# Graph layers of a GNN and expert kernel: node tiles taken in eleven alternating runs, and the weight products dealt out 4, 5, 5, 4

## The reference, cut to what matters

```python
dst = jnp.minimum((6250 * jax.random.uniform(key, (100000,)) ** 2.0).astype(jnp.int32), 49999)
_o = jnp.argsort(dst, stable=True)          # edges come sorted by destination
...
xs = x[src]
seg = dst * R + etype
sums = jax.ops.segment_sum(xs, seg, num_segments=N * R)
cnt = jax.ops.segment_sum(jnp.ones_like(xs[:, 0]), seg, num_segments=N * R)
mean = sums / jnp.maximum(cnt, 1.0)[:, None]
mean = mean.reshape(N, R, -1)
return x @ Wroot + b + jnp.einsum('nrd,rde->ne', mean, W)
```

## Time and profile before

| what | value |
|---|---|
| timed, median of 3 runs | 3500.47 us (3499.16 to 3519.07) |
| span of the profiled execution | 3064.4 us |
| timed median less the span | 436.1 us |
| PE, DVE, POOL busy | 2352.2, 1782.2, 1836.5 us |
| setup, to PE's first matmul of the first layer | 97.4 us |
| first graph layer, from there to its last means | 97.4 to 1191.0 |
| second graph layer, from its first gather to its last means | 1202.6 to 2280.0 |
| routing and experts | from 2280 to the end |

### The profile page before, as it was taken

The page is one execution under the profiler, slowest core; times in us unless marked ns, Lnnn a source line. Parts: engine busy times, 40 slices in busy tenths (PEclk is TensorE's granted clock), DMA queues, the critical chain, the costliest instruction groups (busy, mean ns, idle before and its releaser), DMA issues.

```text
span 3064.4 us, 82720 instructions
## 1 busy us (share of the span) xinstructions
PE 2352.2 (77%) x19212; PEld 1776.0 (58%) x19213; DVE 1782.2 (58%) x4944; ACT 1167.6 (38%) x2306; POOL 1836.5 (60%) x1908
## 2 busy tenths in 40 slices
PE   1456777778888887456777888888987189999999
PEld 0123444555666775123445556667776178888888
DVE  7434445555566664333445555656666278877777
ACT  5001223334445553011223344455542165655554
POOL 1777777766666553777777777666536623333333
PEclk9556789999999998557899999999995599999999
DMA  7343333333333321333343444333335432322222
GB/s 244 100 130 105 108 108 108 109 101 99 97 94 93 90 88 58 106 99 115 115 119 118 123 122 125 112 113 111 106 110 192 146 123 86 100 72 72 72 72 61
DMA packets 164416, 331.14 MB, mean 108 GB/s; under 512 B 35518, under 2 KB 101786, under 8 KB 164216
## 3 DMA queue, kind: packets, MB, share of 16 engines
q0 software_dynamic: 90864, 245.38, 26.9%
q1 hardware_dynamic: 39608, 41.02, 4.5%
q10 hardware_dynamic: 33872, 43.92, 4.5%
HBM read 283.29 MB, written 49.07 MB: 108 GB/s over the span
## 4 chain that ended last, share of the span: by engine, by line
PE 48%; POOL 24%; issue 15%; DVE 7%; DMA 3%; DVEq 2%; ACT 1%; POOLq 0%; SPq 0%; ACTq 0%
POOL ring L450 20%; PE more_banks L1254 15%; PE sum_banks L1392 8%; PE sum_banks L1234 7%; PE sum_banks L1235 5%; PE sum_banks L1382 4%; PE more_banks L1382 4%; POOL lot_in L470 3%; PE more_banks L1246 3%; DMA ring<-table,row_tab 2%; DVE sel L890 1%; DMA out<-edge_work,lot_ids 1%; PE more_banks L1366 1%; DVEq L881 1%; DVE weights L1072 0%
## 5 line engine op out<-in xcount | busy, mean ns | idle before, releaser
L450 POOL DMA_INDIRECT ring<-table,row_tab x1568 | 1509.2, 963 | 703.8 <-issue 339.0
L1254 PE MATMUL more_banks<-weights,stage 128*128 128x256 f16 x5292 | 846.9, 283 | 7.8 <-ACT stage L561 4.5
L589 ACT ACTIVATE stage<-sum_banks,inv 128x256 f16<-128x256 f32 x784 | 327.4, 471 | 815.5 <-DVE inv L923 398.7
L1254 PEld LDWEIGHTS more_banks<-weights,stage 128*128 128x128 f16 x5292 | 502.4, 101 | 144.9 <-issue 71.6
L1234 PE MATMUL sum_banks<-ring,sel 128*128 x1568 | 449.3, 287 | 161.1 <-DVE sel L890 84.2
L898 DVE TENSOR_SCALAR sel_more<-lane,win_off,key_tab 128x128 f16 x780 | 268.8, 345 | 443.4 <-SPq L355 371.2
L1234 PE MATMUL sum_banks<-ring,sel_more 128*128 x780 | 244.3, 314 | 350.0 <-DVE sel_more L898 193.8
L890 DVE SCALAR_TENSOR_TENSOR sel<-lane,win_off,key_tab 128x256 f16<-128x256 f16 x792 | 349.4, 482 | 240.4 <-PE more_banks L1254 235.8
L1235 PE MATMUL sum_banks<-ring,sel 128*128 x1568 | 448.7, 287 | 0.0
L561 ACT ACTIVATE stage<-more_banks 128x1024 f16<-128x1024 f16 x392 | 402.7, 1027 | 15.1 <-PE more_banks L1246 14.9
L1234 PEld LDWEIGHTS sum_banks<-ring,sel_more 128*128 x780 | 78.4, 100 | 529.7 <-issue 524.9
(11 more groups left out here) (287 smaller groups left out, 2763.0 us busy)
## 6 DMA issues: line engine op xcount, KB each, us to landing
ring<-table,row_tab POOLq DMA_INDIRECT x1568
weights<-L_ffn_W ACTq DMA_DIRECT2D x96, 178.5 KB
stage<-L_ffn_W ACTq DMA_DIRECT2D x16, 1024.0 KB, 5.5
edge_work<-lot_in SPq DMA_DIRECT2D x54, 260.0 KB, 2.7
table<-edge_work SPq DMA_DIRECT2D x7, 896.0 KB, 4.4
table<-edge_work ACTq DMA_DIRECT2D x49, 128.0 KB
out<-acc SPq DMA_DIRECT2D x6, 1024.0 KB
acc<-x SPq DMA_DIRECT2D x6, 896.0 KB, 11.0
```

The costliest lines, as they stand in the source:

```text
L450: pool.indirect_dma_start(ring_rows[:, b % RING, 0:2 * D], None, tables[layer], bass.IndirectOffsetOnAxis(row_tab[:, b:b + 1], 0)).then_in ...
L589: act.activation(mean16[:, slot, h, 0:D], ps_sum[slot][h][:, 0:D], ACT.Copy, scale=inv[:, ds(c * 2 + h, 1)]).then_inc(mean_high[layer], 1)
L1254: return [pe.matmul(ps_out[par], rows[:, xp * KD + k, :], w16[:, wp, k, r * D:(r + 1) * D], start=part == 0 and n == 0, stop=part == PARTS ...
```

## The change

1. **Order of tiles.** The tiles are placed in `acc` and in all later work in the order of eleven runs, low and high node numbers in turn. Each run's blocks are gathered as a range of their own; a block that straddles a border of runs is gathered twice, so there are 794 gathers instead of 784. In setup, two tables of 784 columns are copied run by run with eleven copies each on ACT, `free_meta` run by run with eleven operations on DVE, all at places read from registers. Loads of x, stores of `tables[0]` and of the output are cut at the borders.
2. **Products.** The 18 products are dealt 4, 5, 5, 4 over couples 2 and 3 of the next tile and couples 0 and 1 of the one after. The root parts come first. The wait for the means moves to the start of couple 2. Sums, ReLU and the stores of rows come one couple later.
3. **Register arithmetic.** `meta` holds `lo + 2`, called `need`; a gather b goes to slot (b + 2) % 16, so that `need & 15` is the slot. Semaphore values are masked before they are waited for. `lot_meta` becomes 16 bits wide.

```diff
+    RUNS = ((0, 1), (13, 25), (1, 2), (25, 32), (2, 4), (32, 38), (4, 7), (38, 43), (7, 10), (43, 49), (10, 13))
+    COUNT = len(RUNS)
+    AT = [sum(b - a for a, b in RUNS[:r]) for r in range(COUNT + 1)]
+    GATHERS = BLOCKS + COUNT - 1
+    MASK = (1 << (GATHERS + 3 * WINDOWS).bit_length()) - 1
+    PART_ORDER = [R * KD + k for k in range(KD)] + list(range(R * KD))
+    SHARES = (5, 4, 4, 5)
+    SPREAD = {4: (1, 1, 0, 1, 1), 5: (1, 1, 1, 1, 1)}
+    CUTS = (0, SHARES[2], SHARES[2] + SHARES[3], SHARES[2] + SHARES[3] + SHARES[0], PARTS)
...
# POOL
-                for b in range(BLOCKS):
+                for b in range(GATHERS):
...
-                    pool.indirect_dma_start(ring_rows[:, b % RING, 0:2 * D], None, tables[layer],
+                    pool.indirect_dma_start(ring_rows[:, (b + 2) % RING, 0:2 * D], None, tables[layer],
...
# ACT, in setup (and the same for key_tab)
+            for r in range(COUNT):
+                act.activation(row_tab[:, ds(run_to[r], BLOCKS)], row_src[:, ds(run_from[r], BLOCKS)], ACT.Copy).then_inc(tabs_set, 1)
+                act.wait_ge(tabs_set, r + 2)
...
# DVE, in setup
+            for r in range(COUNT):
+                link(v.tensor_scalar(free_row[:, ds(to[r], BLOCKS)], free_src[:, ds(of[r], BLOCKS)], run_steps[:, r:r + 1], run_end[:, r + 1:r + 2], ALU.add, ALU.min))
...
# DVE, more_blocks
-                        v.wait_ge(rows_ready[layer], block + 1)
+                        v.wait_ge(rows_ready[layer], (lo & MASK) + i + 3)
...
# DVE, tile_work
-                        if k == 1 and age == 2:
+                        if k == 2 and age == 2:
                             sums_out(t - 2, par)
...
# PE
-                            pe.wait_ge(more_ready[layer], since + i + 1)
-                            block = (lo + i + 2).with_bounds(min_val=0, max_val=BLOCKS - 1)
-                            add_block(to, flat(sel_more[:, ds(block & (RING - 1), 1), :]), block, False, True).then_inc(steps_done[layer], 1)
+                            pe.wait_ge(more_ready[layer], (since & MASK) + i + 1)
+                            add_block(to, flat(sel_more[:, ds((need + i) & (RING - 1), 1), :]), need + i + 2, False, True).then_inc(steps_done[layer], 1)
...
-                    if k == 0:
-                        parts = [(par, n) for n in range(PARTS - 5, PARTS)] if age == 2 else []
-                    else:
-                        parts = [(1 - par, n) for n in (range(0, 2), range(2, 8), range(8, 13))[k - 1]] if age > 0 else []
-                    spread = ((1, 1, 1, 1, 1), (0, 0, 0, 0, 2), (1, 1, 1, 1, 2), (1, 1, 1, 1, 1))[k]
+                    due = (k + 2) % STEPS
+                    of, enough = (par, age == 2) if k < 2 else (1 - par, age > 0)
+                    parts = [(of, n) for n in PART_ORDER[CUTS[due]:CUTS[due + 1]]] if enough else []
+                    spread = SPREAD[SHARES[k]]
...
+                    if k == 2 and age > 0:
+                        if age == 1:
+                            pe.wait_ge(w_split, layer + 1)
+                        pe.wait_ge(means_in[layer], t * STEPS)
...
-                        pe.wait_ge(rows_ready[layer], lo[j] + 2)
+                        pe.wait_ge(rows_ready[layer], need[j] & MASK)
...
-                    if k == 1 and age > 0:
-                        if age == 1:
-                            pe.wait_ge(w_split, layer + 1)
-                        pe.wait_ge(means_in[layer], t * STEPS)
```

More of the change, by code:

```diff
@@ L67, in build_program, with pieces, whole @@
     WAYS = CHUNK + 1
-    STORES = (TILES - 1) // 8 + 1
-    assert (TILES - 1) % 8 == 0
+    def pieces(first, last):
+        cuts = [(max(AT[r], first), min(AT[r + 1], last)) for r in range(COUNT)]
+        return [(a, b, ORDER[a]) for a, b in cuts if a < b]
+    def whole(first, last):
+        return [p for p in pieces(first, min(TAIL, last)) + pieces(max(TAIL + 1, first), last)]
+    STORES = len(whole(0, TILES)) + 1
     tables = [nc.dram_tensor(f"table{l}", [NP, 2 * D], f16, kind="Internal").ap() for l in range(2)]
@@ L467, in _ @@
                     t = c * CHUNK + i
-                    rows = LAST if t == TILES - 1 else P
+                    rows = LAST if t == TAIL else P
                     for k in range(2):
@@ L855, in _ @@
             v.memset(meta[0:1, 0:1, :], 0)
-            link(v.memset(meta[0:1, WINDOWS:, :], 0))
-            v.tensor_copy(meta[0:1, 0:WINDOWS, 0], lo)
+            link(v.memset(meta[0:1, WINDOWS:, :], 2))
+            for r in range(COUNT):
+                wins = slice(AT[r] * WPT, AT[r + 1] * WPT)
+                v.tensor_scalar(meta[0:1, wins, 0], lo[:, wins], run_shift[:, r:r + 1], 2.0, ALU.add, ALU.add)
+                last = AT[r + 1] * WPT
+                v.tensor_scalar(run_end[:, r + 1:r + 2], upto[:, last - 1:last], 2.0 * last, None, ALU.add)
             v.tensor_copy(meta[0:1, 1:WINDOWS + 1, 1], upto)
@@ L1013, in _ @@
                 v.memset(cells[:, 0:5, :], 0.0)
-            for i in range(CHUNK):
-                v.tensor_scalar(ids7[:, i:i + 1], part_no[:], float(i * P), None, ALU.add)
             v.tensor_scalar(valid, part_no[:], float(LAST), None, ALU.is_lt)
@@ L1176, in _ @@
         def _(pe):
-            pe.wait_ge(consts, 10)
+            pe.wait_ge(consts, 9)
             pe.wait_ge(wrong_ready, 1)
@@ L1199, in _ @@
             pe.wait_ge(later_ready, 1)
-            for a in range(2):
-                for q in range(Q):
-                    ins = pe.matmul(bank[4 + a][:, 0:WINDOWS], ones16[0:NAT, :], later[:, a, q, :], start=q == 0, stop=q == Q - 1)
+            for q in range(Q):
+                ins = pe.matmul(bank[4][:, 0:LOOKS], ones16[0:NAT, :], ends_later[:, q, :], start=q == 0, stop=q == Q - 1)
+            ins.then_inc(spans_ps, 1)
+            pe.wait_ge(later_ready, 2)
+            for q in range(Q):
+                ins = pe.matmul(bank[5][:, 0:WINDOWS], ones16[0:NAT, :], starts_later[:, q, :], start=q == 0, stop=q == Q - 1)
             ins.then_inc(spans_ps, 1)
@@ L1312, in _ @@
                 graph_tiles(pe, tile_work)
-                for n in range(PARTS - 5, PARTS):
+                for n in PART_ORDER[CUTS[2]:CUTS[3]]:
+                    product(1, n)
+                turn(COUPLES - 1, 1)
+                for n in PART_ORDER[CUTS[3]:]:
                     ins = product(1, n)[-1]
                 ins.then_inc(out_done[layer], 1)
-                turn(COUPLES - 1, 1)
+                for n in PART_ORDER[:KD]:
+                    product(0, n)
                 pe.wait_ge(means_in[layer], COUPLES)
@@ L1319, in _ @@
                     weights_spread(1)
-                for n in range(PARTS):
+                for n in PART_ORDER[KD:]:
                     ins = product(0, n)[-1]
```

231 lines of the change are left out of this document (162 added, 69 removed).

## The result

The changed kernel takes 3646.8 us (3635.76 to 3653.22, 4 runs) against 3508.1 for the kernel before, timed beside it: a ratio of **1.039 [1.036, 1.042], slower**. The forecast was 3545, at most 3625.

A forecast was written before the change was run, and what follows sets the result against it. Gathers at 1.25 us were taken to bound low tiles, PE's sequencer the later ones. Terms -30 - 10 - 69 + 136 + 15 + 3 = +45 on the median of 3500.5 gave 3545 us, range 3425 to 3625.

The forecast's parts named there:

- order, with its setup: Graph layers: ring's head start cuts waits for gathers, -30 and -10 us; copies ahead of first gather and matmul add +15.
- dealing of the products: Couples of each tile: dealing 4, 5, 5, 4 saves 0.7 us a tile, -69 us, ends -20 and -108.
- arithmetic, with the rest: PE's loop over more steps: longer turns cost +136 us, ends 0 and +230; tails of both layers +3.
- What lies around it, 436 us, is not touched: Time outside the profiled span of 3064.4 us: unchanged, so the +45 is added to the median of 3500.5.
- two more masks, and one more addition or none: Each turn of PE's loop: added instructions at 0.1 us each, +0.2 or +0.3; 780 x 0.2 = 156 us before hiding.
- rival B: PE's loop: additions don't combine as before, a turn is 0.3 us longer, 78 us more, 3623 us; chance 0.15.
- Rival A: PE's loop: sequencer runs ahead, arithmetic is hidden, none of the 136 us is paid, 3409 us; chance 0.18.
- rival C: PE's loop: half the arithmetic's tax is hidden in couples with queued products, 3477 us, about no change; chance 0.17.
- -0.7 us a tile: Couples 1 and 2 of a tile: saving from the new dealing, between 0.2 and 1.1 us.
- Over 98 tiles: All tiles of both layers: the dealing's saving a tile applied to each, -69 us in all.
- as much as that run now waits for gathers: Heavy runs: head start's gain capped by present waits, 9 + 25 = 34 us in low tiles; -30 taken.
- rival D: Order of tiles: ring's head start gives nothing and each border costs its gather, 3610 us; chance 0.08.

The follow-up runs named there:

- e13: e9 with maxima with 0 in place of PE's masks once a window and once a loop: 3093.1 us, ratio 1.009, quiet set.
- e14: e13 with the products dealt 4, 5, 5, 4: 3068.1 us, ratio 1.001 to the kernel before, quiet set.
- e6: Changed kernel with tiles in natural order and the products dealt as before: 3663.3 us, ratio 1.042, with pauses.
- e9: Kernel before with semaphore values masked outside the loops, PE's and DVE's turns kept at 10 and 7 instructions: 3535.9 us, ratio 1.021, with pauses.
- e16: The program of e9 run again in a quiet set: 3146.4 us, ratio 1.027 to the kernel before.
- e10: e9 with PE's turn of the loop at 13 instructions, as in the changed kernel: 3654.8 us, ratio 1.055, with pauses.
- e18: Changed kernel with all tiles in one run in natural order: 3228.2 us, ratio 1.053, quiet set.
- e11: e9 with DVE's turn of the loop at 9 instructions: 3548.3 us, ratio 1.025, with pauses.
- e17: The whole changed kernel run again in a quiet set: 3247.1 us, ratio 1.059 to the kernel before.
- e8: e7 with its tiles in natural order: 3535.7 us, ratio 1.006, with pauses.
- e7: Changed kernel with masks taken out of the two loops and one slot computed for both places, PE's turn 10 instructions: 3572.5 us, ratio 1.016, with pauses.
- e1: Kernel before with its three small integer tables 16 bits wide instead of 32: 3870.0 us, ratio 1.102, with pauses.

## Why the prediction was wrong

| term | forecast | with pauses | quiet |
|---|---|---|---|
| order, with its setup | -40 + 15 | +22 | +19 |
| dealing of the products | -69 | -35 | -25 |
| arithmetic, with the rest | +136 + 3 | about +150 | +187 |
| sum | +45 | +139 | +181 |

The last line and the first two are measured (the quiet dealing between e13 and e14, in a kernel with short turns); the third is what they leave, and e6 measures it directly with pauses (+149). Setup, read from PE's first matmul, is 22 us longer where 15 were forecast: some 15 come with the order and 8 with the arithmetic.

**The footing.** "What lies around it, 436 us, is not touched" was wrong. The difference came with the pauses, and most of it lies inside the layers: e9 takes 394 us more than e16, the same program, 180 in each layer and 33 behind them. The pauses are not the whole of it, since behind the layers e9 has none. The sign that I passed over stood in the head of the case: a span 436 us below the timed figure, where every later trace has a span 2 to 3 us below the time of its own run. It did little harm to the forecast, since the change costs 139 on the one footing and 181 on the other. The three terms failed by themselves.

**The turn of the loop: the mechanism was right, the size and the count too small.** The argument that PE's pace is its sequencer's holds (e10), and so does 0.1 us an instruction in tile 0's loop: three more make 0.28 to 0.33. I had counted "two more masks, and one more addition or none" and took none: +0.2 for a turn that grew by three instructions, the third a move. That is rival B's turn of 1.37. 780 x 0.33 = 257 would be the tax. Of it 187 less 8 of setup is left (DVE's longer turn, below, still in it), so about 78 lie hidden, not 20. Tile 0 of the second layer hides 32 of them: 166.1 us became 172.6 in e18, 6 in place of 38. Tile 0 of the first, from which nothing was to be taken off, hides 17:

```profile
105.20:273.60 168.40, 38.44 (x116) 0.50 0.37 107
```

That is 21 us more than the 147.6 of the earlier trace rows. The rest is spread over tiles 1 to 24, as in tiles 13 to 24 above. So the price of a turn was too low by more than the hiding was. Rival A is refuted in the main: the tax was hidden by less than a third, which is short of rival C's half too. The Trainium skill's "TensorE: Matmul & The Clock Gate" (table at its head) gives TensorE's queue a depth of 64. Windows of e16 and e13, in which products stand beside the steps, still pay 5 to 15 us in 24 tiles for instructions of the sequencer, so here a queue of that depth hides them neither in the loop nor wholly among products.

DVE's longer loop, which the sum put at nothing, is not free: two instructions more in DVE's turn cost 12 us with pauses (e11).

**The dealing: right in one place, spread over too many.** "-0.7 us a tile" is what a light tile of the first layer gains (16 us in 24 tiles). No product waits for ACT any more, as promised. Ends of the couples' transposes in tile 47 of e17, against the earlier trace rows:

```profile
1201.58 0.61 PE L1365 MATMUL more_banks<-ident,stage 128*128 128x128 f16 x8
1204.35 0.61 PE L1365 MATMUL more_banks<-ident,stage 128*128 128x128 f16 x8
1207.22 0.61 PE L1365 MATMUL more_banks<-ident,stage 128*128 128x128 f16 x8
1210.18 0.61 PE L1365 MATMUL more_banks<-ident,stage 128*128 128x128 f16 x8
```

They stand 2.77, 2.87 and 2.96 apart, where they had 3.40 and 2.96. The failed step is "Over 98 tiles". Tiles 0 to 24 gain next to nothing (225.1 us for tiles 13 to 24 with either dealing), I take it because products there lie beside more steps or gathers; the second layer's light tiles gain 0.2 each. The row that I read was from tile 45 of the first layer, and its wait for ACT is not one of 98. In the kernel before PE's matmuls sat idle for ACT in front of products 7 times in both layers, 4.5 us in all (and its weight loads 15 times, 7.5 us):

```profile
PE more_banks L1254 <- ACT stage L561: 4.5, 7, 1.1
```

**The order: the step "as much as that run now waits for gathers" used the kernel before.** The same change that moved the tiles made the turn 1.39 us, above a gather's 1.25. In the heavy tiles PE no longer waits for gathers: one wait of 8.0 us is left, and even in natural order (e18) it is 9.4 us in five waits. So a head start of 16 blocks has little to pay, and nothing came of the 40. The chain after a light run stays clear of POOL, as promised, but that says nothing for the order. In e17 tile 2 and 3 take 85.4 us and the light tile ahead of them 22.4; in e18 91.6 and 15.1: the sums are 107.8 and 106.7. What a heavy run gains the light tile ahead of it loses. So it goes in both layers: tiles 0 to 12 take 29 and 28 us less in e17 than in e18, tiles 13 to 48 take 38 and 32 more. Of rival D the first half came true, the head start gives nothing; its sign did not, as PE was not found waiting for gathers, nor its price, as the twenty more of them stand on an engine with 539 us of waiting.

The longer turn is not the whole reason. With short turns and pauses PE in natural order does wait for gathers (e8: 21.6 us, 23 times), and the order costs 37 us there, more than the 22 with long ones; with it the waits are 31.5 us, 32 times (e7). Why it costs there too stays open. What the order costs is partly setup: the first gather at 86.5 (as forecast) against 79.5 in e18, PE's first matmul at 119.7 (forecast 112) against 105.2:

```profile
119.74 0.39 PE L1354 MATMUL sum_banks<-ring,sels 128*128 x1 [28.69 <-DVE sels L1009]
```

```profile
105.22 0.39 PE L1352 MATMUL sum_banks<-ring,sels 128*128 x1 [16.42 <-DVE sels L1007]
```

From the first gather on, the first layer takes 1213.6 us in e17 and 1197.5 in e18, the second 1152.5 and 1149.4. Some 7 of the 16 are setup that comes after the first gather. Where in the passages the rest lies was not settled, and short turns with the order were not tried in a quiet set.

**The sum.** Adding the three edits was right: with pauses the parts add. Each term was off by itself. The arithmetic took two of three instructions a turn, the dealing one row for 98 tiles, and the order took waits that the arithmetic had removed.

## What to carry to other kernels

In a loop whose pace is the sequencer's, every instruction of a turn has a price: count them in the compiled loop, keep masks ahead of it, and bound values with operations that are fused with the adds. Put what must be done once a tile behind queued work, not behind the load of its registers. Before a row is multiplied by the number of tiles, count how often it stands there; before a wait is counted as a gain, see whether another edit takes it away; and hold the span of the trace against the timed figure before anything else: if they differ, look for the longest register instruction.

## What the runs showed that I had not expected

- The same program takes 12 to 15% longer in some sets than in others: 3064.6 us against 3461 to 3514 for the kernel before, 3146 against 3536 for e16 and e9. In the traces register instructions of PE, DVE and SP now and then take 0.7 us, in turns or together. They are not all of it: in the last 24 tiles of the first layer e9 has 5 of them and takes 23 us more than e16, and behind the layers it has none and takes 33 more. The Trainium skill's "Runtime: NRT & Kernel Launch" ("Instruction fetch mechanics") tells of stalls of a sequencer after a taken branch whose target is not among the instructions that it has at hand. The traces bear out that cause only in so far as the pauses lie in the layers, which have the loops; they fall on adds in the midst of a turn, and e16, the same program as e9, has none. The cause stays open.
- Loading 20 registers of PE from a table of 16 bits takes 4.73 us, from 32 bits 1.36 (e1 and the changed kernel).
- The changed kernel loses more where there are no pauses (181 against 139 us), and the kernel with the new dealing alone and fused bounds is level with the kernel before (e14, 1.001). No kernel here beats the kernel before.
